# Expert layer of a vision block: tokens as the stationary operand of the second product, in 14 of 16 blocks

## The chip, the cores and the metric

The kernel runs on one core of a Trainium2 chip. The metric is the device time of one execution in microseconds (us), and the time before is the median of three runs, 1112.26 us (1110.14 to 1114.20).

## The reference

Four images of 64 channels and 64x64 pixels go through three layers, each added to or built on the one before:

```python
h = tok(x)                                  # dynamic 3x3 depthwise filter, result (4, 4096, 64)
h = h + attn(layernorm(h))                  # one head over 4096 tokens of width 64, softmax of scores
h = h + ffn(layernorm(h))                   # router picks 1 of 32 experts for each token

# ffn, for all tokens n:
idx = argmax(xf @ router_w.T + router_b)            # E = 32 experts
h   = relu(einsum('nd,ndh->nh', xf, W1[idx]) + b1[idx])    # H = 16 hidden values
out = relu(einsum('nh,nhd->nd', h, W2[idx]) + b2[idx])     # D = 64 values
```

The change is in the last line, the second product of the experts. All is in float32.

## The kernel before, in words

The 16384 tokens are worked on in 16 blocks of 1024 (`BLOCKS`, four to an image). The array is used as four quarters of 64x64 throughout: a helper `rows_of(r)` picks partitions 64r to 64r+63, and the rows (contraction) and columns (output partitions) of a product choose the quarter. In what follows a record is one MATMUL of the trace; a float32 product leaves two records, each with its own LDWEIGHTS, and a bf16 product one.

Attention sets the frame. Each block n has 16 groups g; in each, TensorE makes scores (`score`, L789, 16 records of 64x512), ScalarE takes the exponential (L1009), and TensorE weighs the keys with it (`into_z`, L800, 16 records of 64x512). All other work of TensorE is a list of "fills", named as `o2@7` (fill o2 of block 7), which a hand-written plan (`opening_groups` to `last_groups`) puts at a group of a block. TensorE, ScalarE and VectorE all walk through the same plan in the same order. In `group`, TensorE issues the scores of group g, then the fills of that group, then the weighing of group g-1. The fills of group 16 of a block stand after the last scores of that block and ahead of the first scores of the next one.

All fills of the blocks that the change touches write to one pair of PSUM banks, `both` (128 partitions, 2 banks of 512 float32). A fill waits until the fill before it in that place has been drained (`wait_free`).

The expert layer of a block is a chain of fills. `ot` turns the one-hot choice; `hid0` to `hid3` are the first product, in four slices of 128 of the 32x16 = 512 hidden rows, and stand by hidden row with tokens along the free axis. In blocks 3 to 13 VectorE drains them (L1233) with relu and the mask of the chosen expert; in blocks 0 to 2 ScalarE does (L1001). `o2` is the second product: `w2` and `b2_parts` are stationary, the tokens stream past in runs of 512 columns, and the sums stand by output channel, tokens along the free axis (L763, L771). VectorE adds the two banks into `o2_sb` (L1274, L1278). `fin`, in the next block, is the way back: 16 products with an identity matrix turn 64x64 pieces of `o2_sb` so that tokens lie on partitions (L779). VectorE then does relu and adds the residual (`put_out`, L1201), and SyncE stores the block (`store_block`, L399), waiting for the drain of `fin` (L404). Behind that store on SyncE's queue stand the loads of dynamic filters for a later block (`spread_filters`).

Ahead of blocks 4, 8 and 12 all engines pass a branch, `shift_if_needed` (L860): TensorE waits on several semaphores (L918 to L921), loads a flag and branches on it (L862). In the usual plan `o2@7` and `o2@11` are the last fills ahead of such a branch; ahead of block 4 it is a convolution (`cv@9`, L697).

The last two blocks (14 and 15) have a plan of their own with other PSUM places.

Of the kernel before, what the change touches and what calls it, by code (L numbers as in the profile page):

```python
# [22 lines left out]
BT = QB // 128  # L23
# [62 lines left out]
def at(i, names):  # L86
    return [f"{n}@{i}" for n in names.split()] if 0 <= i < BLOCKS else []
# [53 lines left out]
def third_groups():  # L141
    return {-1: at(1, "z"), 0: at(0, "lg"), 2: at(0, "ot"), 3: at(1, "pz"), 4: [*at(0, "hid0"), *at(6, "sum2 ln")],
            5: at(0, "hid1"), 6: at(0, "hid2"), 7: at(0, "hid3"), 8: at(1, "yt"), 9: at(0, "o2"), 10: at(1, "lg"),
            11: at(6, "xt"), 12: at(6, "g"), 13: [*at(1, "ot"), *at(7, "sum0 sum1")], 14: at(0, "fin"),
            15: at(1, "hid0"), 16: at(1, "hid1")}


def fourth_groups():
    return {-1: at(2, "z"), 0: at(1, "hid2"), 1: at(1, "hid3"), 2: at(2, "pz"), 3: at(1, "o2"), 4: [*at(9, "cc"), *at(7, "sum2 ln")],
            5: at(2, "yt"), 6: at(2, "lg"), 7: at(1, "fin"), 8: at(7, "xt"), 9: at(7, "g"),  # L150
            10: [*at(2, "ot"), *at(8, "sum0 sum1")], 11: at(2, "hid0"), 12: at(2, "hid1"), 13: at(2, "hid2"),
            14: at(2, "hid3"), 15: at(2, "o2"), 16: at(9, "cv")}


def usual_groups(n):

    m, i, j = n - 1, n + NQ, n + NQ + 1
    pair = {4: at(j + 1, "cc"), 7: at(j + 1, "cv")} if j + 1 in PAIRED else {}
    groups = merged({-1: at(m, "z"), 1: at(m - 1, "fin"), 2: at(m, "pz"), 4: at(i, "sum2"), 5: at(m, "yt"),
                     6: at(m, "lg"), 7: at(i, "ln")}, pair,  # L160
                    {8: at(m, "ot"), 9: at(i, "xt"), 10: [*at(i, "g"), *at(j, "sum0 sum1")]})
    if m in CHOSEN_BY_DMA:
        return merged(groups, {12: at(m, "hid0"), 13: at(m, "hid1"), 14: at(m, "hid2"), 15: at(m, "hid3"), 16: at(m, "o2")})
    return groups
# [40 lines left out]
def vit_block_kernel(nc, x, once, kept, out):  # L205
# [6 lines left out]
    with ExitStack() as ctx:  # L212
# [181 lines left out]
        def _(sp):  # L394
# [3 lines left out]

            def store_block(m):  # L399
                fin = f"fin@{m}"  # L400
                if m == BLOCKS - 2:
                    sp.wait_ge(out_ready, 1)
                else:
                    sp.wait_ge(drained[places.of[fin]], places.nth[fin])  # L404
                for half in range(HH):
                    rows = out.rearrange("b (c h q t) w -> b q h c (t w)", c=C, h=HH, q=NQ)
                    sp.dma_start(rows[m // NQ, m % NQ, half, :, :],
                                 out_sb[half * C:(half + 1) * C, m % 2, :, :].rearrange("c t w -> c (t w)")
                                 ).then_inc(out_stored[m % 2], 16)
# [185 lines left out]
        def _(pe):  # L595
# [36 lines left out]
            def from_both(to, weights, tokens, f, start, stop):  # L632
# [5 lines left out]
                                        start=start, stop=stop)  # L638
                return last

            def begin_hidden(full):
                name, i = split(full)
                wait_free(full)
                wait_drained(f"yt@{i}")
                from_both(place[places.of[full]], w1, y_t, int(name[3:]), start=True, stop=False)

            def fill(full):
# [63 lines left out]
                elif name == "g":  # L711
                    if full == "g@0":
                        wait_drained("aw@0")
                    wait_drained(f"xt@{i}")
                    for r in range(2):
                        for c in range(2):
                            cols = slice(0, 512) if i < NQ else half_of(c)
                            last = T.matmul(both[rows_of(c), r, 0:cols.stop - cols.start],  # L718
                                            a_w[rows_of(r), rows_of(c)],
                                            keys_t[rows_of(r), par, q * 512 + cols.start:q * 512 + cols.stop],  # L720
                                            start=True, stop=True)
                    last.then_inc(done, 1)
                elif name == "pz":
                    pe.wait_ge(z_copied, i + 1)
                    for j in range(BT // 2):
                        for c in range(2):
                            for h in range(2):
                                last = T.matmul(both[rows_of(h), c, j * 65:(j + 1) * 65],  # L728
                                                z_sb[rows_of(c), j * 128 + h * 64:j * 128 + h * 64 + 64],
                                                wv_w[rows_of(c), c * 65:(c + 1) * 65], start=True, stop=True)  # L730
                    last.then_inc(done, 1)
                elif name == "lg":
                    wait_drained(f"yt@{i}")
                    for j in range(BT // 2):
                        for r in range(2):
                            for h in range(2):
                                last = T.matmul(both[rows_of(h), r, j * E:(j + 1) * E],  # L737
                                                y_t[rows_of(r), j * 128 + h * 64:j * 128 + h * 64 + 64],
                                                router_w[rows_of(r), :], start=True, stop=True)
                    last.then_inc(done, 1)  # L740
                elif name == "ot":
                    pe.wait_ge(onehot_ready, i + 1)
                    last = turn([onehot[:, t, :, :].rearrange("p u e -> p (u e)") for t in range(BT)], ident_bf)
                    last.then_inc(done, 1)
                elif name.startswith("hid"):
                    f = int(name[3:])
                    wait_drained(f"ot@{i}")
                    if i == BLOCKS - 1 and f == FT - 1:
                        pe.wait_ge(upper_hidden, 1)
                    ahead = full in AHEAD  # L750
                    if i not in CHOSEN_BY_DMA:
                        last = from_both(mine, mask_w, onehot_t, f, start=not ahead, stop=ahead)
                    if not ahead:
                        last = from_both(mine, w1, y_t, f, start=i in CHOSEN_BY_DMA, stop=True)
                    last.then_inc(done, 1)
                elif name == "o2":
                    if i == BLOCKS - 1:

                        pe.wait_ge(upper_hidden, 2)

                    for part in range(2):
                        for r in range(2):
                            T.matmul(mine[rows_of(r), r, :], b2_parts[rows_of(r), part, :], onehot_t[rows_of(r), :],  # L763
                                     start=(part == 0), stop=False)
                    for f in range(FT):
                        wait_drained(f"hid{f}@{i}")
                        if i == BLOCKS - 1:
                            pe.wait_ge(upper_hidden, f + 1)
                        for h in range(2):
                            for r in range(2):  # L770
                                last = T.matmul(mine[rows_of(r), h, :], w2[rows_of(h), f, :], hidden[rows_of(h), f, r, :],  # L771
                                                start=(f == 0 and h != r), stop=(f == FT - 1))
                    last.then_inc(done, 1)
                else:
                    wait_drained(f"o2@{i}")
                    for j in range(4):
                        for r in range(2):
                            for h in range(2):
                                last = T.matmul(both[rows_of(h), r, j * 64:(j + 1) * 64],  # L779
                                                o2_sb[rows_of(r), j * 128 + h * 64:j * 128 + h * 64 + 64],  # L780
                                                ident[rows_of(r), rows_of(r)], start=True, stop=True)
                    last.then_inc(done, 1)
# [301 lines left out]
        def _(dve):  # L1084
# [120 lines left out]
            def drain(full):  # L1205
# [66 lines left out]
                elif name == "o2":  # L1272
                    if i < BLOCKS - 2:
                        V.tensor_copy(o2_sb[:, :], mine[:, 0, :])  # L1274
                        settle()
                    else:
                        dve.wait_ge(lower_copied, i - (BLOCKS - 3))
                    V.tensor_tensor(o2_sb[:, :], o2_sb[:, :], mine[:, 1, :], ALU.add).then_inc(done, 1)  # L1278
                else:
                    put_out(i, both[:, :, 0:256]).then_inc(done, 1)  # L1280

# [133 lines left out]
```

## Time and profile before

| | |
|---|---|
| median of three runs | 1112.26 us (1110.14 to 1114.20) |
| the profiled execution's own time | 1112.06 us |
| its span in the profile | 1110.3 us |
| mean granted TensorE clock | 0.994 of full speed |
| PE busy | 1087.4 us (98%), 12516 matmul records |
| PEld (weight loads, beside PE) | 560.2 us (50%) |
| DVE / ACT / POOL busy | 527.7 / 583.2 / 13.2 us (48% / 53% / 1%) |
| DMA | 63.43 MB, mean 57 GB/s |

How to read it: busy time of an engine is the time in which at least one of its instructions runs, so with four quarters at work a record of 0.59 us may add only 0.11 us. The span is what the profile covers; the profiled execution's own time is 1.8 us more than its span and 0.2 us below the median.

### The profile page before, as it was taken

To read this page: it belongs to the slowest core of one execution; us is meant where nothing else is said; L and a number is where in the kernel's file an instruction comes from. 1 tells how busy PE (TensorE), PEld (TensorE's weight loads), DVE (VectorE), ACT (ScalarE), POOL (GpSimd) and SP (SyncE) were. 2 spreads that over 40 slices of the span, in tenths; PEclk is the share of its full clock that TensorE was granted. 3 is DMA by queue.
4 is the path that set the end of the run, shared out by engine and by line. 5 is a ranking of instruction groups with operands and counts; after the bars stand their busy time and mean duration, and the time that the engine had idled before them with its cause. 6 is when DMAs were issued, how large, how long until landed. Compare 5 with 4: busy or idle time off the path is not lost.

```text
span 1110.3 us, 28800 instructions
## 1 busy us (share of the span) xinstructions
PE 1087.4 (98%) x12516; PEld 560.2 (50%) x12516; DVE 527.7 (48%) x1039; ACT 583.2 (53%) x657; POOL 13.2 (1%) x44
## 2 busy tenths in 40 slices
PE   7899999999999999999999999999999999999997
PEld 4244444555444555555555455555545555554543
DVE  7868765436064553735547364553523131312305
ACT  2466656556555464545546465464645545454543
POOL 3100000000000000000000000000000000000000
PEclk9899999999999999999999999999999999999999
DMA  4845621113025140222313023240100101010000
GB/s 107 198 112 131 135 66 35 40 39 78 5 68 119 39 108 20 62 70 68 83 40 91 19 69 80 47 101 11 39 15 11 42 12 41 11 40 3 12 1 20
DMA packets 23057, 63.43 MB, mean 57 GB/s; under 512 B 3934, under 2 KB 8382, under 8 KB 22540
## 3 DMA queue, kind: packets, MB, share of 16 engines
q1 hardware_dynamic: 22364, 61.26, 23.1%
q8 instruction: 103, 1.69, 0.7%
q10 hardware_dynamic: 560, 0.23, 0.1%
q14 instruction: 30, 0.25, 0.1%
HBM read 52.87 MB, written 5.47 MB: 53 GB/s over the span
## 4 chain that ended last, share of the span: by engine, by line
PE 95%; DVE 2%; issue 1%; DMA 1%; ACT 1%; DVEq 0%; PEld 0%; PEldq 0%; SPq 0%
PE z_ps L800 40%; PE scores L789 38%; PE both L637 5%; PE both L771 4%; PE both L628 2%; PE both L779 1%; PE both L737 1%; PE both L718 1%; PE both L728 1%; PE both L697 1%; PE both L685 1%; DMA filter_ring<-filters 1%; PE both L763 0%; PE scores L637 0%; DVE hres L1173 0%
## 5 line engine op out<-in xcount | busy, mean ns | idle before, releaser
L1009 ACT ACTIVATE probs<-scores 128x1024 f32<-128x1024 f32 x512 | 496.4, 1021 | 464.3 <-PE scores L789 464.3
L789 PE MATMUL scores<-g_t,keys_t 64*64 64x512 f32 x4096 | 513.9, 591 | 2.3 <-ACT g_t L988 1.2
L800 PE MATMUL z_ps<-probs,keys 64*64 64x512 f32 x4096 | 510.5, 591 | 0.0
L789 PEld LDWEIGHTS scores<-g_t,keys_t 64*64 64x64 f32 x4096 | 222.3, 134 | 226.7 <-issue 220.7
L800 PEld LDWEIGHTS z_ps<-probs,keys 64*64 64x64 f32 x4096 | 207.4, 133 | 178.9 <-issue 171.8
L1233 DVE SCALAR_TENSOR_TENSOR hidden<-both,chosen 128x1024 f32<-128x1024 f32 x44 | 53.9, 1225 | 200.6 <-PE both L637 189.3
L1173 DVE TENSOR_TENSOR hres<-hres,tap_product 128x504 f32<-128x504 f32 (+1 forms) x128 | 87.8, 686 | 11.2 <-issue 0.9
L1161 DVE SCALAR_TENSOR_TENSOR tap_product<-filter_ring,w,xin 128x504 f32<-128x504 f32 (+1 forms) x117 | 87.0, 743 | 8.1 <-DMA filter_ring<-filters 4.4
L637 PE MATMUL both<-y_t,w 64*64 64x512 f32 x448 | 61.4, 589 | 0.0
L771 PE MATMUL both<-hidden,w 64*64 64x512 f32 x448 | 56.9, 592 | 0.0
L1274 DVE COPY o_sb<-both 128x512 f32<-128x512 f32 x14 | 9.7, 691 | 85.2 <-PE both L771 85.2
L1191 DVE COPY z_sb<-z_ps 128x512 f32<-128x512 f32 x14 | 9.7, 692 | 68.2 <-PE z_ps L800 68.2
L1141 DVE TENSOR_REDUCE stat<-logits 128x8 f32<-128x256 f32 x16 | 6.7, 420 | 64.2 <-ACT logits L994 64.2
L637 PEld LDWEIGHTS both<-y_t,w 64*64 64x64 f32 x448 | 23.4, 133 | 22.4 <-issue 21.7
L771 PEld LDWEIGHTS both<-hidden,w 64*64 64x64 f32 x448 | 24.1, 133 | 20.5 <-issue 19.7
L1262 DVE RECIPROCAL stat<-both 128x8 f32<-128x8 f32 x16 | 3.3, 208 | 57.4 <-PE both L728 57.4
L1121 DVE TENSOR_TENSOR tap_product<-tap_product 128x512 f32<-128x512 f32 x32 | 22.2, 692 | 2.4
L1123 DVE TENSOR_REDUCE stat<-tap_product 128x8 f32<-128x512 f32 x32 | 21.9, 686 | 2.3
L628 PEld LDWEIGHTS both<-w,keys 64*64 64x64 f32 x512 | 11.5, 134 | 14.8 <-issue 14.8
L779 PEld LDWEIGHTS both<-w,o_sb 64*64 64x64 f32 x512 | 13.2, 134 | 9.4 <-issue 9.4
L628 PE MATMUL both<-w,keys 64*64 64x64 f32 x512 | 11.2, 219 | 6.8 <-DVE keys L1130 6.8
L1201 DVE SCALAR_TENSOR_TENSOR out_sb<-both,h 128x256 f32<-128x256 f32 x30 | 11.3, 420 | 13.1 <-PE both L779 13.1
(162 smaller groups left out, 557.5 us busy)
## 6 DMA issues: line engine op xcount, KB each, us to landing
filter_ring<-filters SPq DMA_DIRECT2D x88, 384.0 KB, 5.4
chosen<-choices SPq DMA_DIRECT2D x44, 256.0 KB
out_dram<-out_sb SPq DMA_DIRECT2D x32, 128.0 KB, 2.4
xin<-x_dram SPq DMA_DIRECT2D x6, 528.0 KB, 9.7
g_t<-g_t SPq DMA_DIRECT2D x24, 128.0 KB, 6.1
hidden<-once_dram SPq DMA_DIRECT2D x1, 930.0 KB, 14.4
chosen<-filters SPq DMA_DIRECT2D x2, 384.0 KB, 6.8
choices<-onehot_t SPq DMA_DIRECT2D x22, 32.0 KB, 1.6
```

The source lines that it names most:

```text
L628: last = T.matmul(both[rows_of(a), h, j * 64:(j + 1) * 64], tiles[2 * j + a][rows_of(h)], ident[rows_of(h), rows_of(h)], start=True, stop= ...
L637: last = T.matmul(to[rows_of(c), r, :], weights[rows_of(r), cols], tokens[rows_of(r), :], start=start, stop=stop)
L771: last = T.matmul(mine[rows_of(r), h, :], w2[rows_of(h), f, :], hidden[rows_of(h), f, r, :], start=(f == 0 and h != r), stop=(f == FT - 1))
L779: last = T.matmul(both[rows_of(h), r, j * 64:(j + 1) * 64], o2_sb[rows_of(r), j * 128 + h * 64:j * 128 + h * 64 + 64], ident[rows_of(r), r ...
L789: last = T.matmul(scores[rows_of(h), c, r * 512:(r + 1) * 512], keys_t[rows_of(r), i // NQ % 2, k * 128 + 64 * h:k * 128 + 64 * h + 64], g ...
L800: last = T.matmul(z_ps[rows_of(c), h, :], keys[rows_of(h), i // NQ % 2, 2 * k + r, :], probs[rows_of(h), (2 * g + c) % RING, r * 512:(r + ...
L1009: A.activation(probs[:, unit % RING, :], scores[:, c, :], ACT.Exp, scale=SCALE).then_inc(probs_ready, 1)
L1121: V.tensor_tensor(squares[:, :, :], centred[:, :, :], centred[:, :, :], ALU.mult)
L1123: V.reduce_sum(total, squares[:, :, :], AX_X)
L1161: return V.scalar_tensor_tensor(dst[:, :, lo:hi], flt, keep["b2c"][:, t:t + 1], pix, ALU.add, ALU.mult)
L1173: V.tensor_tensor(mine[:, :, lo:hi], mine[:, :, lo:hi], dst[:, :, lo:hi], ALU.add)
L1233: V.scalar_tensor_tensor(hidden[:, f, :, :], place[k][:, :, :], 0.0, chosen[:, f, :, :], ALU.max, ALU.mult).then_inc(drained[k], 1)
```

## The change

In blocks 0 to 13 the operands of the second product are swapped. A new function `experts_by_token` makes, for each of 4 token runs j and 2 halves r, first the bias (4 bf16 products, one-hot stationary, `b2_parts` moving, 64 columns) and then 16 float32 products with 64 tokens of `hidden` stationary and `w2` (64 columns) moving. Its sums stand by token in `both`. The fill `fin` goes out of the plan for these blocks. VectorE adds the two banks as before and then calls `put_out` on `o2_sb` at once, and SyncE waits for that through `out_ready`. Blocks 14 and 15 are as they were.

```diff
@@ def third_groups():
-            11: at(6, "xt"), 12: at(6, "g"), 13: [*at(1, "ot"), *at(7, "sum0 sum1")], 14: at(0, "fin"),
-            15: at(1, "hid0"), 16: at(1, "hid1")}
+            11: at(6, "xt"), 12: at(6, "g"), 13: [*at(1, "ot"), *at(7, "sum0 sum1")], 15: at(1, "hid0"), 16: at(1, "hid1")}
@@ def fourth_groups():
-            5: at(2, "yt"), 6: at(2, "lg"), 7: at(1, "fin"), 8: at(7, "xt"), 9: at(7, "g"),
+            5: at(2, "yt"), 6: at(2, "lg"), 8: at(7, "xt"), 9: at(7, "g"),
@@ def usual_groups(n):
-    groups = merged({-1: at(m, "z"), 1: at(m - 1, "fin"), 2: at(m, "pz"), 4: at(i, "sum2"), 5: at(m, "yt"),
+    groups = merged({-1: at(m, "z"), 2: at(m, "pz"), 4: at(i, "sum2"), 5: at(m, "yt"),
@@ def store_block(m):
-                if m == BLOCKS - 2:
-                    sp.wait_ge(out_ready, 1)
+                if m < BLOCKS - 1:
+                    sp.wait_ge(out_ready, m + 1)
@@ TensorE
+            def experts_by_token(i):
+
+
+                def to(bank, c, r, j):
+                    return both[rows_of(c), bank, 256 * r + 64 * j:256 * r + 64 * j + 64]
+
+                def tokens(c, j):
+                    return slice(128 * j + 64 * c, 128 * j + 64 * c + 64)
+
+                for f in range(FT):
+                    wait_drained(f"hid{f}@{i}")
+                for j in range(BT // 2):
+                    for r in range(2):
+                        for part in range(2):
+                            for c in range(2):
+                                T.matmul(to(r, c, r, j), onehot_t[rows_of(r), tokens(c, j)], b2_parts[rows_of(r), part, :],
+                                         start=(part == 0), stop=False)
+                        for f in range(FT):
+                            for h in range(2):
+                                for c in range(2):
+                                    last = T.matmul(to(h, c, r, j), hidden[rows_of(h), f, r, tokens(c, j)],
+                                                    w2[rows_of(h), f, :], start=(f == 0 and h != r), stop=(f == FT - 1))
                 return last
@@ fill o2
+                    if i < BLOCKS - 2:
+                        experts_by_token(i).then_inc(done, 1)
+                        return
@@ VectorE, drain of o2
                     V.tensor_tensor(o2_sb[:, :], o2_sb[:, :], mine[:, 1, :], ALU.add).then_inc(done, 1)
+                    if i < BLOCKS - 2:
+                        settle()
+                        put_out(i, o2_sb[:, :].rearrange("p (r n) -> p r n", r=2)).then_inc(out_ready, 1)
```

## Rows read from the trace of the kernel before

**Rows 1.** The page's part 4, the chain that ended last, by engine.

```profile
PE 95%; DVE 2%; issue 1%; DMA 1%; ACT 1%; DVEq 0%; PEld 0%; PEldq 0%; SPq 0%
```

**Rows 2.** Groups of instructions by form: shapes, count | busy us, mean ns | idle before.

```profile
L771 PE MATMUL both<-hidden,w 64*64 64x512 f32 x448 | 56.9, 592 | 0.0
...
L779 PE MATMUL both<-w,o_sb 64*64 64x64 f32 x512 | 14.0, 220 | 1.6 <-DVE o_sb L1278 1.6
...
L763 PE MATMUL both<-onehot_t,b_parts 64*64 64x512 bf16 x56 | 9.0, 376 | 0.0
```

**Rows 3.** Chain in order of time, 745 to 830 us: start us, us, what.

```profile
759.77 0.17 PE both L763
...
760.20 3.43 PE both L771 x30
...
767.07 1.35 PE scores L789 x15
768.41 0.07 PE both L779 x3
...
769.19 1.78 PE z_ps L800 x16
770.97 1.66 PE scores L789 x15
```

**Rows 4.** Timeline of PE, 740 to 815 us: start us, us, instruction, count.

```profile
781.47 1.98 PE L789 MATMUL scores<-g_t,keys_t 64*64 64x512 f32 x16
783.18 0.67 PE L628 MATMUL both<-w,y_block 64*64 64x64 f32 x30
...
785.37 1.98 PE L789 MATMUL scores<-g_t,keys_t 64*64 64x512 f32 x16
...
792.70 1.98 PE L789 MATMUL scores<-g_t,keys_t 64*64 64x512 f32 x16
...
796.31 1.96 PE L789 MATMUL scores<-g_t,keys_t 64*64 64x512 f32 x16
```

**Rows 5.** Timeline of PE, 334.5 to 338 us, where PE had waited ahead of L628.

```profile
336.82 0.69 PE L628 MATMUL both<-w,keys 64*64 64x64 f32 x32
337.31 1.07 PE L800 MATMUL z_ps<-probs,keys 64*64 64x512 f32 x8
```

**Rows 6.** Waits: who for whom, us in total, times, longest us.

```profile
PEld both L763 <- DVE hidden L1233: 6.1, 11, 0.6
```

**Rows 7.** Timeline of DVE, 758 to 776 us; in brackets the idle time before.

```profile
758.16 1.23 DVE L1233 SCALAR_TENSOR_TENSOR hidden<-both,chosen 128x1024 f32<-128x1024 f32 x1 [3.07 <-PE both L637]
...
767.10 0.69 DVE L1191 COPY z_sb<-z_ps 128x512 f32<-128x512 f32 x1 [1.98 <-PE z_ps L800]
```

**Rows 8.** Chain in order of time, 298 to 304 us, the branch ahead of block 4.

```profile
301.38 0.77 issue
302.15 1.90 PE scores L789 x13
```

**Rows 9.** PE's sequencer (PEldq), one line each, 298 to 304 us: duration, first and last start.

```profile
L921 PEldq EVENT_SEMAPHORE  x2: 51/51/51, 300.3 to 300.4; - x2
```

**Rows 10.** The same of 560 to 570 us, the branch ahead of block 8.

```profile
L921 PEldq EVENT_SEMAPHORE  x2: 51/51/51, 563.7 to 563.8; - x2
...
L809 PEldq EVENT_SEMAPHORE  x1: 51/51/51, 565.4 to 565.4; - x1
```

**Rows 11.** Chain in order of time, 562 to 568 us, the same branch.

```profile
563.02 3.43 PE both L771 x30
```

**Rows 12.** One line of the source, 765 to 770 us: its wait behind fin.

```profile
L819 PEldq EVENT_SEMAPHORE  x1: 51/51/51, 768.8 to 768.8; - x1
```

**Rows 13.** One line of the source, 765 to 770 us: fin's own records.

```profile
L779 PE MATMUL both<-w,o_sb x32: 216/218/268, 768.2 to 769.0; 64*64 64x64 f32 x32
```

**Rows 14.** The page's part 3: the queue of instructions; packets, MB, share.

```profile
q8 instruction: 103, 1.69, 0.7%
```

**Rows 15.** Waits of SyncE's queue.

```profile
SPq L407 <- DVE out_sb L1201: 421.2, 15, 72.2
```

More of the change, by code:

```diff
@@ L639, in from_both @@
                 return last
+            def experts_by_token(i):
[16 more added lines that the diff above has]
+                                                    w2[rows_of(h), f, :], start=(f == 0 and h != r), stop=(f == FT - 1))
+                return last
             def begin_hidden(full):
```

## The prediction

> **What bounds the kernel now.** I read the page's shares first, then the chain that ended last: 95% of the span is TensorE's [rows 1]. The chain in order of time shows why nothing else counts: through a block it goes from one group of matmul records to the next without a hole. So every us of TensorE's stream taken out or put in shows in the time, wherever it stands, and the other engines matter only where they make TensorE wait. I then took the widths of the fills from the timeline and the queue's behaviour from TensorE's sequencer. All is costed against the profiled execution's own time, 1112.06 us (span 1110.3 and 1.8 around it), 0.2 below the median.
>
> **A pace to work with.** A group of 16 attention records takes 1.716 us on the chain; with four quarters at work that is 0.429 us for a 512-column float32 record in its quarter. Scores that begin at 781.47 and 785.37 have between them themselves, one weighing and the 32 float32 records of 64 columns of a turn: 3.90 - 3.43 = 0.47 us [rows 4], or 8 records in each quarter at 0.0585 us, 14.6 ns a record over all. In the same way the 16 bf16 records of 64 columns between 792.70 and 796.31 cost 0.18 us [rows 4].
>
> **1. What goes, 4.34 us a block.** From the end of one weighing at 759.77 to the scores at 770.97 the chain takes 11.20 us and holds four attention groups (6.86), o2 and fin [rows 3]: 4.34 us for the two. It splits into 3.43 of w2 records, 0.43 for two 512-column bf16 records in sequence in two of the quarters (759.77 to 760.20), and 0.47 for fin, a turn like that above. The counts, 448, 56 and 512 records [rows 2] (the last holds blocks 14 and 15 as well), are 32, 4 and 32 a block, and they are the same in all 14 blocks. Gone: 14 x 4.34 = 60.8 us.
>
> **2. What comes, 4.08 us a block.** 8 times (j, r) there are 16 float32 products, 32 records of 64 columns, in the same round of four quarters as a turn: 256 records, 8 x 0.468 = 3.74 us. The bias is 32 bf16 records, 8 in each quarter. Below: 512 bf16 columns take 0.215 us where float32 takes 0.429, so half of 0.0585, 8 x 0.029 = 0.23, total 3.98. Above: 14.6 ns for each of the 288 records whatever its kind, 4.20; two turns of the bf16 kind, 0.36, lie between. I take 0.34: 0.23 and, four times in each quarter, some 0.027 because the float32 weights that follow a bf16 record take longer to load than that record runs. Coming: 14 x 4.08 = 57.1 us. Parts 1 and 2 make -3.7 us, with ends -5.0 and -2.0. The products do the same arithmetic; what is saved is fin and the long bias, and what eats it is that a 64-column record costs a little more than an eighth of a 512-column one.
>
> **3. The waits ahead of it, +0.10 us in 11 blocks.** Before, one wait stood ahead of o2, and its record could sit in the queue with others behind it; TensorE's loads waited up to 0.6 us for VectorE's last hidden drain in all 11 blocks where VectorE drains [rows 6], which ended at 758.16 + 1.23 = 759.39 [rows 7], just before the weighing ran out, so it cost almost nothing. Now five waits stand ahead of the first record. An instruction carries one and the sequencer takes the others, two at a time, so it stands still until 759.4, with an empty queue behind. Where it had stood still before a turn, records came at once and at full pace: 32 from 336.82 to 337.31, 0.49 against 0.47 [rows 5]. Two waits of 0.05 with the gap between them, the load and the start put the first record near 759.67 instead of 759.56. Ends: 0 and 0.25. With 0.10, 11 x 0.10 = 1.1 us. Blocks 0 to 2 have their drains done earlier: nothing.
>
> **4. The branch behind it, +1.65 us twice.** The sequencer runs ahead of the array by a fixed stock of instructions, not of time. Ahead of block 8 it was at the waits of L921 at 563.7 and through the branch at 565.4, while o2's long records ran until 566.45: the branch cost nothing [rows 10, 11]. Ahead of block 4 a shorter fill stood there, the sequencer came to L921 at 300.3, scores began at 302.15, 1.85 later, and the chain has a hole of 0.77 [rows 8, 9]. Behind 64-column records the stock is worth little time: behind fin the sequencer was at its next wait at 768.8, 0.2 before fin's last record started [rows 12, 13]. So ahead of blocks 8 and 12, where o2@7 and o2@11 are the last fills, 1.85 - 0.20 = 1.65 us of hole opens each time, 3.3 us. Ends: 0 (the stock still covers it) and 3.7. Ahead of block 4 nothing changes. At other blocks' starts only one or two waits follow o2, as behind fin, where the stream went on unbroken: nothing.
>
> **5. The rest, nothing.** VectorE's put_out (two instructions of 0.42) moves from behind fin to behind o2; VectorE was idle there for 1.98 us ahead of the z copy at 767.10 [rows 7], and o2's banks are still freed by the add ahead of it. If that cover were gone, the z copy has until pz, a group and a half later. pz now waits for o2 instead of fin, drained long before. On SyncE the store of a block waited for put_out 421.2 us in all [rows 15]; it goes some 4 us earlier, and so may the filter loads behind it, as far as their own wait for free slots (`filters_used`) lets them; they feed VectorE's sums, which don't set the end. More instructions are fetched: 14 x (576 - 136) = 6160 beside some 25000, a quarter more than the 103 packets now [rows 14], one packet in about 1.9 us through the new stretch.
>
> **Sum.** -60.8 + 57.1 + 1.1 + 3.3 = +0.7 us: 1112.8 from the profiled execution, 1113.0 from the median.
>
> **Rivals.**
> *Supply (slower).* The longest run of 64-column records in the trace is 32, which the stock may partly hold; the new one has 288 (576 instructions). If the sequencer or the fetch can't keep 14.6 ns a record, the run goes at its pace. The slowest such run here, fin's on the chain from 768.41 to 769.19, 0.78 us for 32 [rows 3], is 24 ns a record: 288 x 24 = 6.9 us, 14 x (6.9 - 4.34) = +36, with parts 3 and 4 1153 us. It decides from 14.8 ns on: 4.26 us a block make -1.1, with the 4.4 of parts 3 and 4 +3.3, slower by 0.3%. For it: no long run was ever seen, and an instruction packet would have to come in 1.9 us. Against: the run of rows 5 started with the sequencer standing still and still kept the pace; and fin's slowness is a skew that the long bias had left between the quarters (the scores ahead of it count 1.35 on the chain instead of 1.72 [rows 3]). Chance 0.12.
> The Trainium skill, page "TensorE: Matmul & The Clock Gate", section "Wait — 56ns, not 53.3ns?", says that matmuls never start closer than about 25 ns; by it the new stretch would take 7.2 us a block and the kernel 1157 us, as an estimate from that page. The 14.6 ns of [rows 4] contradict it for runs of 32 over four quarters, so I give it no more than the chance of this rival.
> *Upper ends (slower).* The stretch at 4.20 us a block, 0.25 at the start, 1.85 at both branches: -2.0 + 2.8 + 3.7 = +4.5, 1116.8 us. Mechanism: the short stock of instructions, in both places. Chance 0.18.
> *Lower ends (faster).* The bias in its own time, the waits under the skew of the quarters, the sequencer still ahead at the branch: -5.0, 1107.2 us. For it: the branch was hidden at both places before. Against: [rows 8, 12]. Chance 0.17.
>
> **How the numbers follow.** My own case has 0.53. What a measurement tells from no change is about 0.3%, 3.3 us, here 1109 to 1115.6. Faster is the lower ends, 0.17; slower the supply and the upper ends, 0.30; the same 0.53. The range goes from the lower ends, 1107.5, past the upper ends to a supply that is a little short (15.6 ns a record, 4.50 us a block, +6.7), 1119; the likeliest case alone is 1110 to 1115.
>
> **What would show it.** Between the last scores ahead of o2 and the next, the new stretch should be 4.0 to 4.2 us wide, with 256 float32 and 32 bf16 records; L779 should be left with 64 records; the attention groups should keep their 1.716 us. Ahead of blocks 8 and 12 the chain should have an "issue" hole of 1.1 to 1.7 us where it had none, and the first record of the stretch should start 0.1 us after the last hidden drain is through. A stretch over 4.3 us, a hole inside it, or no hole at the branches would make the forecast wrong.

## The result, and the profile after

The changed kernel takes 1157.33 us in the median of four runs (1155.78 to 1160.97), against 1112.77 for the kernel before in the same comparison: a ratio of 1.0399, 95% interval 1.0380 to 1.0418. It is 4% slower; 1113.0 was forecast with a range to 1119. The profiled execution took 1155.78 us (span 1154.0), 43.7 more than that of before. In the kernel after, L655 and L660 are the bias and the products of the new stretch, L815 the scores, L826 the weighing, L888 the branch and L805 the way back that blocks 14 and 15 still have.

One correction to the names in the forecast: a block's plan holds the expert fills of the block before it, so the last fills ahead of the branches of blocks 8 and 12 are o2@6 and o2@10, not o2@7 and o2@11. The places in the traces are the ones that were read; only the numbers were wrong.

First the page's part 4, shares of the chain; it answers to [rows 1].

```profile
PE 92%; issue 3%; DVE 2%; DMA 1%; ACT 1%; PEld 0%; DVEq 0%; PEldq 0%; SPq 0%
```

"issue" is time in which TensorE waited for nothing that the profile shows. It was 1% and is 3%, some 35 us against 11. The groups by form say where (count | busy us, mean ns | idle before), to be laid beside [rows 2]:

```profile
L660 PE MATMUL both<-w,hidden 64*64 64x64 f32 x3584 | 64.6, 221 | 17.5 <-issue 17.5
...
L655 PE MATMUL both<-b_parts,onehot_t 64*64 64x64 bf16 x448 | 26.8, 191 | 4.3 <-issue 4.3
...
L805 PE MATMUL both<-w,o_sb 64*64 64x64 f32 x64 | 1.4, 220 | 1.6 <-DVE o_sb L1304 1.6
```

The counts are the forecast ones (14 x 256 = 3584, 14 x 32 = 448, 64 left of the way back), but inside the new stretch TensorE stood idle for 21.8 us. One stretch on the chain in order of time (start us, us, what), the place that answers to [rows 3]:

```profile
789.06 0.49 PE both L660 x30
789.55 0.01 PE both L655
...
790.08 0.38 PE both L660 x18
790.46 1.45 issue
791.90 0.45 PE both L660 x12
...
792.84 0.07 PE both L660 x3
792.91 1.72 PE scores L815 x14
794.63 1.72 PE z_ps L826 x16
```

Up to 790.08 each unit of 36 records (one pair j, r of the new function: 4 of the bias and 32 of the products) takes 0.51 us, 14.2 ns a record, the forecast pace. Then nothing is issued for 1.45 us, and afterwards the pace is the same again. Every one of the 14 stretches has such a hole, and two have two; from the start of the record before to the start of the record after they measure 1.1 to 1.9 us and 25.2 us in all.

The stretch ahead of block 8 (it stands at o2@6) is one of those with two, and runs into the branch:

```profile
577.33 1.50 issue
...
580.92 1.68 issue
582.60 0.62 PE both L660 x24
...
584.71 3.03 issue
587.74 3.69 PE scores L815 x16
```

From the last product at 583.22 to the first scores at 587.74 are 4.5 us, where the long records of o2 had hidden the branch whole [rows 11]. (The chain lays part of that hole on VectorE's drain of o2, which ran beside it.) The sequencer's branch instruction itself, over the kernel (duration min/median/max; the maximum is the first branch, at 20 us):

```profile
L888 PEldq COMPARE_BRANCH  x4: 342/3640/5274, 20.5 to 862.2; - x4
```

The same of the kernel before:

```profile
L862 PEldq COMPARE_BRANCH  x4: 323/339/4811, 20.2 to 827.0; - x4
```

Before, the three later ones took 0.35, 0.32 and 0.33 us. The one ahead of block 4 is still short now (0.34), the two behind new stretches take 3.5 and 3.7. A clock loss follows both: the scores at 587.74 take 3.69 us instead of 1.72. By stretch (us, busy of PE, PEld, DVE, ACT, POOL, PEclk, DMA):

```profile
588.00:597.00 9.00, 9.00 (x64) 2.85 (x63) 1.38 (x2) 3.99 (x4) 0.00 (x0) 0.74 0.40 90
866.40:875.00 8.60, 8.60 (x68) 3.00 (x72) 1.38 (x2) 3.99 (x4) 0.00 (x0) 0.84 0.01 3
```

TensorE is busy throughout, and the granted clock, 1.00 at these places before, is at its lower level of 1.2 GHz for part of the time: 9.0 x 0.26 + 8.6 x 0.16 = 3.7 us lost, after holes of 4.5 to 5 us that followed stretches which had each stood idle twice.

### The profile page after: what moved, and what is told of

Read it like the earlier page. It is cut to its first block, busy times and chain, and to the rows that moved or that the text cites. A ratio compares the mean times of both kernels' runs of the same rounds, so it can differ in the third digit from the quotient of the medians.

```text
span 1154.0 us, 34976 instructions
## 1 busy us (share of the span) xinstructions
PE 1100.1 (95%) x15596; PEld 484.7 (42%) x15596; DVE 527.1 (46%) x1039; ACT 583.5 (51%) x657; POOL 13.1 (1%) x44
## 4 chain that ended last, share of the span: by engine, by line
PE 92%; issue 3%; DVE 2%; DMA 1%; ACT 1%; PEld 0%; DVEq 0%; PEldq 0%; SPq 0%
PE z_ps L826 38%; PE scores L815 38%; PE both L660 5%; PE both L636 4%; PE both L627 1%; PE both L741 1%; PE both L751 1%; PE both L760 1%; PE both L720 1%; PE both L708 1%; DMA filter_ring<-filters 1%; PE scores L636 0%; DVE hres L1199 0%; PEld both L929 0%; PE z_ps L797 0%
## 5 line engine op out<-in xcount | busy, mean ns | idle before, releaser
L815 PE MATMUL scores<-g_t,keys_t 64*64 64x512 f32 x4096 | 500.1, 596 | 13.1 <-issue 11.9
L826 PE MATMUL z_ps<-probs,keys 64*64 64x512 f32 x4096 | 496.3, 593 | 0.0
L815 PEld LDWEIGHTS scores<-g_t,keys_t 64*64 64x64 f32 x4096 | 172.2, 134 | 282.1 <-issue 267.0
L826 PEld LDWEIGHTS z_ps<-probs,keys 64*64 64x64 f32 x4096 | 161.3, 134 | 229.7 <-issue 199.4
L660 PE MATMUL both<-w,hidden 64*64 64x64 f32 x3584 | 64.6, 221 | 17.5 <-issue 17.5
L660 PEld LDWEIGHTS both<-w,hidden 64*64 64x64 f32 x3584 | 60.5, 134 | 19.3 <-issue 19.3
L655 PE MATMUL both<-b_parts,onehot_t 64*64 64x64 bf16 x448 | 26.8, 191 | 4.3 <-issue 4.3
L636 PEld LDWEIGHTS both<-y_t,w 64*64 64x64 f32 x448 | 18.8, 133 | 27.1 <-issue 26.2
L655 PEld LDWEIGHTS both<-b_parts,onehot_t 64*64 64x64 bf16 x448 | 20.1, 107 | 13.4 <-DVE hidden L1259 7.1
L627 PEld LDWEIGHTS both<-w,keys 64*64 64x64 f32 x512 | 11.0, 139 | 14.4 <-issue 14.4
L1187 DVE SCALAR_TENSOR_TENSOR hres<-filter_ring,w,xin 128x512 f32<-128x512 f32 x15 | 11.3, 756 | 12.4 <-DMA filter_ring<-filters 9.3
```

What stands on the lines that cost most here:

```text
L627: last = T.matmul(both[rows_of(a), h, j * 64:(j + 1) * 64], tiles[2 * j + a][rows_of(h)], ident[rows_of(h), rows_of(h)], start=True, stop= ...
L636: last = T.matmul(to[rows_of(c), r, :], weights[rows_of(r), cols], tokens[rows_of(r), :], start=start, stop=stop)
L655: T.matmul(to(r, c, r, j), onehot_t[rows_of(r), tokens(c, j)], b2_parts[rows_of(r), part, :], start=(part == 0), stop=False)
L660: last = T.matmul(to(h, c, r, j), hidden[rows_of(h), f, r, tokens(c, j)], w2[rows_of(h), f, :], start=(f == 0 and h != r), stop=(f == FT - 1))
L815: last = T.matmul(scores[rows_of(h), c, r * 512:(r + 1) * 512], keys_t[rows_of(r), i // NQ % 2, k * 128 + 64 * h:k * 128 + 64 * h + 64], g ...
L826: last = T.matmul(z_ps[rows_of(c), h, :], keys[rows_of(h), i // NQ % 2, 2 * k + r, :], probs[rows_of(h), (2 * g + c) % RING, r * 512:(r + ...
```

## The experiments

My theory after the two traces (S): the supply of instructions. TensorE's queue of instructions moves packets of 16 KB (q8: 103 packets before, 128 after). 25 more packets for the 6160 more instructions is about 250 in each, so I took a packet for 256; 576 instructions at 7 ns each ask for packets faster than they come. The expectations below call what one packet holds a block of instructions, and where it ends a block boundary. Rivals: a hazard of the new product itself, its sums, banks or waits (H); a floor under the pace (P); packets that happen to be held up by other transfers (D).

**1. A meter: runs of plain products in the kernel before.** The same tile, constant operands, the result overwritten, so no sums and no new waits; only length and width differ.

```diff
+METER = {3: (64, 64), 4: (64, 128), 5: (64, 192), 6: (64, 288), 7: (64, 512), 8: (128, 288), 9: (128, 512),
+         10: (256, 288), 11: (64, 1024), 12: (96, 512), 13: (128, 1024)}     # block: (columns, records)
+                    if i in METER:                                            # ahead of the bias of o2
+                        columns, records = METER[i]
+                        for k in range(records // 8):
+                            for h in range(2):
+                                for c in range(2):
+                                    T.matmul(both[rows_of(c), h, 0:columns], ident[rows_of(h), rows_of(h)],
+                                             w1[rows_of(h), 0:columns], start=True, stop=True)
```

> The kernel before, with runs of plain 64x64 float32 products (constant operands, result overwritten) put ahead of the bias of o2 in blocks 3 to 13; columns and records: 64/64, 64/128, 64/192, 64/288, 64/512, 128/288, 128/512, 256/288, 64/1024, 96/512, 128/1024. Each record is two instructions. Theory S (instruction supply): TensorE holds two blocks of 256 instructions, and one that is asked for when its predecessor is entered can be used about 3.5 us later. Then 64-column records keep 14.6 ns until the second block boundary inside a run and stall 1.7 us there and at each later one: no hole at 64 records, none or one at 128 and 192, one or two at 288, three at 512, seven at 1024 (some 27 us instead of 15). With 96 columns (21 ns a record) holes of about 0.8 us; with 128 columns (28 ns a record, 3.6 us per 256 instructions) next to none whatever the length, with 256 columns none. Rival H (a hazard of the new product: its sums, banks or waits): plain products have none of these, so no holes at any length. Rival P (a floor on the pace of 25 ns a record): no holes, but every 64-column run at 25 ns, 7.2 us for 288.

The timeline of PE in that run (start us, us, line and shapes, count, idle before): the 1024 records of 64 columns, then 1024 of 128 columns.

```profile
957.49 4.01 PE L767 MATMUL both<-w 64*64 64x64 f32 x259
962.86 2.09 PE L767 MATMUL both<-w 64*64 64x64 f32 x128 [1.36 <-issue]
966.33 2.09 PE L767 MATMUL both<-w 64*64 64x64 f32 x128 [1.38 <-issue]
969.80 2.09 PE L767 MATMUL both<-w 64*64 64x64 f32 x128 [1.38 <-issue]
973.27 2.09 PE L767 MATMUL both<-w 64*64 64x64 f32 x128 [1.38 <-issue]
977.29 2.09 PE L767 MATMUL both<-w 64*64 64x64 f32 x128 [1.93 <-issue]
980.76 2.03 PE L767 MATMUL both<-w 64*64 64x64 f32 x123 [1.38 <-issue]
...
1125.69 28.68 PE L767 MATMUL both<-w 64*64 64x128 f32 x1024
```

This is the cause in one view. A hole comes after every 128 records, that is 256 instructions, one packet; from the end of one hole to the end of the next are 3.47 us (once 4.02). With records twice as wide (28.4 us for 1024, 27.8 ns each, 3.55 us for 256 instructions) not one hole opens in 1024 records. The other runs, with holes now measured from the start of the record before to the start of the record after, which is 0.2 us more than the idle time: 64, 128 and 192 records of 64 columns none (0.92, 1.89 and 2.84 us, 14.4 to 14.8 ns each); 288 one of 1.5; 512 three of 1.6, 1.9 and 1.9, 3.74 and 3.75 us apart; 96 columns two of 1.4 and 1.1; 128 columns with 288 and 512, and 256 columns, none. H falls, since plain products do it, and P, since between holes the pace is 14.7 ns. D falls as the main cause too. All that moved while the run of 1024 went on, from 950 to 990 us, were nine instruction packets:

```profile
DMA packets 9, 0.15 MB, mean 4 GB/s; under 512 B 0, under 2 KB 0, under 8 KB 0
## 3 DMA queue, kind: packets, MB, share of 16 engines
q8 instruction: 9, 0.15, 1.4%
```

I had expected seven holes and got six, since the first two boundaries of the run passed free instead of one; the next hole, 128 records on, fell into the bias of o2 right behind the run (1.06 us of idle time at 983 us).

**2. The same stretch in three pieces.** In 11 blocks the units stand at three groups, with attention between them.

```diff
+PIECES = {"outa": range(0, 3), "outb": range(3, 5), "o2": range(5, 8)}     # units (j, r)
+    late = {0: at(m - 1, "outb"), 1: at(m - 1, "o2")} if m - 1 in CHOSEN_BY_DMA else {}
-        ... 16: at(m, "o2")
+        ... 16: at(m, "outa")
```

> The changed kernel, but in blocks 3 to 13 the eight units of the new product are made in three pieces of 3, 2 and 3 units (216, 144 and 216 instructions), at group 16 of the block and groups 0 and 1 of the next, with two attention groups between pieces. Same products, same instructions, same waits. Theory S: no piece holds two block boundaries, so the holes of 1.1 to 1.9 us go in these 11 blocks (13 holes, about -20 us), the holes at the branches ahead of blocks 8 and 12 and the low clock behind them shrink (about -10 us and more), and the three early blocks keep theirs: about 1125 us. Rival H: the holes stay where the sums or banks make them, about 1157. Rival D (transfers that happen to delay single packets): holes stay at random places, above 1150.

Measured: 1126.91 us, ratio 1.0120 (1.0096 to 1.0145), so 30 us less than the whole stretch for the same instructions. All 13 holes of those 11 blocks are gone. Ahead of block 8 the chain reads:

```profile
572.49 0.49 PE both L662 x31
572.99 2.23 issue
575.22 3.64 PE scores L819 x16
```

The branch instruction took 1.25 us there, 0.92 more than the 0.33 it takes at best, so the rest of the hole, 1.3 us, is the short stock of my step 4 (forecast 1.65), now seen without the supply on top. Ahead of block 12 the same sum gives 1.3 again (a hole of 2.68, a branch of 1.70). The scores behind it again take twice their time.

**3. The changed kernel without the branches.**

```diff
-                    shift_if_needed(b)          # TensorE, ahead of blocks 4, 8 and 12; ScalarE and VectorE alike
```

> The changed kernel without the guard ahead of images 2 to 4 (the branches of blocks 4, 8 and 12 on all engines are left out; the work that they skip is skipped anyway). Theory S: the 16 holes inside the stretches stay (some 24 us), the holes behind the stretches of blocks 7 and 11 (4.8 and 5.0 us) go, with them the two spells of half clock behind them (about 3 us each) and the 2.4 us hole in block 4: about 1139 us. My forecast's step on the branch (1.65 us twice): 1154. Rival: the low clock comes from the stretches and not from the branch holes: about 1145.

The first branch, at 20 us, stays. Measured: 1136.80 us, ratio 1.0228 (1.0195 to 1.0262), 20.5 us less than with them; the four runs lie between 1134.54 and 1141.07, so this is good to a few us. The holes in the stretches stayed (16 again, at other records, since the packets' boundaries moved); mean clock of the profiled run 0.995 instead of 0.986. So a third to a half of the loss of 44.6 us is the branches with what hangs on them, far more than the 3.3 us of the forecast.

**4. The product over all 128 partitions.** Half as many float32 products, two halves of the array side by side.

```diff
+                        for part in range(2):
+                            for c in range(2):
+                                T.matmul(to[c], onehot_t[:, tokens[c]], b2_tall[:, r, part, :], start=(part == 0), stop=False)
+                        for f in range(FT):
+                            for c in range(2):
+                                last = T.matmul(to[c], hidden[:, f, r, tokens[c]], w2[:, f, :], start=False,
+                                                stop=(f == FT - 1))
```

> The second product with tokens stationary as in the change, but with all 128 partitions as the contraction (a tile of 128 rows by 64 columns), so that 16 products of a unit become 8, and the two banks need no adding. 192 records instead of 288 (384 instructions instead of 576), each two records of a column half side by side. Theory S: the array needs 128 records x 29 ns = 3.74 us and 64 x 15 for the bias, 4.1 to 4.7 us, and in 3.7 us of it only 256 instructions are used, so the supply just keeps up: holes of 0 to 0.5 us instead of 1.1 to 1.9; with the branches some 1118 to 1128 us. Rival P or H: the stall goes with the change of operands and stays, above 1145. If records of this shape run at 0.117 us in place of 0.0585, 3.7 us more a block, about 1165.

I had miscounted: a unit has 16 + 4 records, so there are 160 and 320 instructions, not 192 and 384. Measured: 1128.39 us, ratio 1.0146 (1.0122 to 1.0170). The float32 part of a unit on the chain:

```profile
769.33 0.49 PE both L663 x16
769.82 0.06 PE both L660 x4
769.88 0.49 PE both L663 x16
```

Half as many records in the same 0.49 us, no hole in any of the 14 stretches: what stalls is the count of instructions in a time, not the arithmetic. But the bias takes longer in this form, the whole is 4.5 us wide and gains nothing on the 4.34 of before, blocks without a branch behind them are 0.47 us longer than before, and behind it the branches still stalled (3.1 and 2.3 us for the instruction).

**5. Blocks 6 and 10 as before, the others changed.** Three kernels: the pieces of 2 in blocks 3 to 5, 7 to 9 and 11 to 13, with 0 to 2 as before too; whole stretches in all 12; the product of 4 in all 12.

```diff
+BY_TOKEN = (3, 4, 5, 7, 8, 9, 11, 12, 13)                                    # pieces
+BY_TOKEN = tuple(i for i in range(BLOCKS - 2) if i not in (6, 10))           # whole; 128 partitions
```

> The new product in three pieces (3, 2 and 3 units) in nine blocks (3 to 5, 7 to 9, 11 to 13); the second product and the way back as before in blocks 0 to 2 and in blocks 6 and 10, whose fills stand ahead of the branches. Theory S: no hole anywhere, no branch hole: what is left is the array's own side of my forecast, -0.2 us a block, so about 1111 us, 0.997 to 1.000 of before. If the pieces cost at their edges (a wait, a skew) what they save, 1113. If splitting only hides part of the stall, 1120 or more.

> The changed kernel, whole stretches, but blocks 6 and 10 as before, so that 3.5 us of long records stand ahead of the branches of blocks 8 and 12. Theory S: saved are both stretches (6.8 us), both branch holes (9.5) and the half clock behind them (some 6): about 1135 us. Rival (the branch holes come from where the block boundaries happen to fall, not from the stretch ahead): only the 6.8 us go, about 1150.

> The product over all 128 partitions in 12 blocks, blocks 6 and 10 as before. In the run with all 14 its stretch had no hole but was 4.47 us wide and more with the bias, and blocks without a branch took 64.72 us against 64.25 before. Theory S: the branch holes (4.05 and 3.1 us) go, 12 x 0.47 us stay: about 1118 us. If the holes at the branches stay, 1125.

Whole stretches: 1138.12 us, ratio 1.0221 (1.0203 to 1.0240), 19 us saved by two blocks out of 14; 22 had been expected, and some 7 if the stretch ahead of a branch had no part in its hole. Over 128 partitions: 1119.64, ratio 1.0058 (1.0041 to 1.0075). Pieces: 1111.37 us over 12 runs, ratio 0.9988 (0.9978 to 0.9999), the only version that is not slower than the kernel before; it is 0.1% faster, which barely leaves the interval. Its chain at one block shows the array's side of the forecast free of the supply:

```profile
629.22 0.04 PE both L661 x2
...
630.80 1.72 PE scores L823 x16
632.52 1.71 PE z_ps L834 x16
634.24 0.03 PE both L661 x2
...
635.26 1.72 PE scores L823 x16
636.98 0.03 PE both L661 x2
...
638.53 1.62 PE z_ps L834 x11
```

The pieces take 1.58, 1.02 and 1.55 us: 4.15 for 288 records, where 4.08 was forecast for the stretch and 4.34 stood before.

The later branches of this kernel took 0.22 to 0.35 us. In the kernel with whole stretches they took 0.35, 1.07 and 0.33, in that over 128 partitions 0.35, 1.22 and 0.33, and in the meter the one ahead of block 8 took 3.52 and opened a hole of 3.05 us, although 3.5 us of o2's long records stood between it and the run of 288. So a fast stretch makes a long branch likely, and a packet's boundary at the wrong place can, it seems, still do it without one right ahead. That the kernel before had three short ones may in part be luck of where its boundaries fall; I have not moved its boundaries alone to prove it.

## Why the prediction was wrong

**Step 1, what goes (4.34 us a block): right.** The way back is gone from the trace, and most blocks of the kernel in pieces are shorter by 0.22 us than those before, where steps 1 and 2 make 0.26.

**Step 2, what comes (4.08 us, ends 3.98 and 4.20): right for the array.** 4.15 us in pieces; in the whole stretches it is 4.1 to 4.3 us once the hole is taken off.

**Step 3, the waits ahead (+0.10): nothing.** As at 786.97 on the chain, the stretch follows what stands ahead of it without a hole in all 14 blocks. The five waits are all on one semaphore, and in blocks 3 to 13 the trace has only one instruction of the sequencer ahead of the stretch, with two waits, and one more wait at the first weight load.

**Step 4, the branch (+1.65 twice): right mechanism, wrong size.** 1.3 us is what the short stock costs (experiment 2). On top the branch itself took 3.2 and 3.4 us more than at best, and behind the holes the clock fell, 3.7 us. Ahead of block 4, where nothing was to change, a hole of 1.83 us opened just behind the branch. These make some 15 us; taking the branches out gave 20.5 (experiment 3). Of the rest, 0.8 is the hole that the kernel before has too at the branch of block 4 [rows 8], and in the profiled runs 3.2 us of the difference stand in the opening, ahead of the first branch taken out. So the branches cost 15 to 20 us, not 3.3.

**Step 5 and the rival "supply": the step that failed.** "One packet in about 1.9 us through the new stretch" stood there as costing nothing, and the rival that doubted it had a chance of 0.12. Its price, 1153 us, came near, but for another reason than the one I gave it: I let it slow every record to 24 ns, by the record pace of a fill whose slowness was skew, while the pace stays at 14.2 ns (14.7 in the meter) and the time goes in whole holes, 25.2 us in 16 of them. And what I held against it, [rows 5], proved nothing on supply: the 64 instructions of a turn pass one boundary at most. The number that decided was in the forecast, 1.9 us a packet; what was missing was how long a packet takes to be of use. The trace before would have given a warning: packets came some 10 us apart, nowhere were 128 records made in less than 5.6 us, and where two packets followed each other most closely, behind the branches of blocks 8 and 12, they started 3.5 and 3.4 us apart.

**The sum.** In start-to-start times, profiled run against profiled run: 25 us of holes in the stretches; 9.6 from the last product to the next scores at the two branches (4.8 and 5.0, against none); some 2 at the branch of block 4; 3.7 of low clock behind the branches; -1.4 to -2.7 for the array's own gain. That makes 38 to 39 of the 43.7. Another 2 us stand in the opening, where the mean clock from 30 to 70 us was 0.84 instead of 0.90. They need not come from the change: the kernel in pieces of experiment 5, whose blocks 0 to 2 are as before, is 2.5 us longer in the opening too. The remaining 3 to 4 us, in blocks 4, 9 and 14 above all, I have not placed.

**A right total with a wrong mechanism.** The Trainium skill, page "TensorE: Matmul & The Clock Gate", section "Wait — 56ns, not 53.3ns?", with its floor of 25 ns between matmuls would have given 1157 us, the measured time to the us, and is still not the cause: between holes the records start 14.7 ns apart in runs of 128 (experiment 1). A right total is no proof of the mechanism. The page of the Trainium skill that does bear on it is "Runtime: NRT & Kernel Launch", section "Instruction fetch mechanics": instructions come in blocks of 16 KiB (256), fetched one ahead while the current one runs. The traces agree with the block (a hole per 128 records of two instructions). The same section of the Trainium skill says that the fetch is mostly hidden, because the sequencer dispatches more slowly than it fills; here it is not, at 7.4 ns an instruction (14.7 for a record of two). And it says that a taken branch whose target lies outside the two blocks at hand forces a fetch; the long branches of 3.5 and 3.7 us fit that, against 0.33 for a short one, but no run here moved a branch's target alone.

## What to carry to other kernels

Count instructions per time as well as columns per time: in the runs of this kernel TensorE could use 256 instructions in less than about 3.5 us (13.7 ns each) only for the length of one packet or two, and beyond that a hole followed at every further packet, of some 3.5 us less the time that the packet's instructions ran. The 3.5 is an estimate between the 3.47 us of the run with holes and the 3.55 of the run without. So many small float32 products, four instructions each, should be spread between long ones in pieces of fewer than 256 instructions, or made with a larger contraction so that one instruction does more. And nothing fast should stand right ahead of a branch: the sequencer's lead is a number of instructions, and what was hidden behind 3.5 us of long records costs its time behind short ones (1.3 us here, and with a long branch 4.5 to 4.7).

## What the runs showed of the hardware that was not expected

- At full demand 256 instructions take 3.47 us, holes included, four times of five in the run of 1024 records (once 4.02), 3.74 and 3.75 in the run of 512 and 3.74 in the run with 96 columns. Only packets of instructions moved in all three, so why the longer ones are longer is open. Records of 128 columns show no hole at 3.55 us per 256.
- The first boundary or two of a run pass free: in the meter the first hole came after 159, 180 and 259 records of 64 columns and after 298 of 96, the later ones every 128. That the sequencer was ahead there, or that these packets were asked for in the slow part, is my reading and not shown.
- A tile of 128 rows by 64 columns takes as long per column half as one of 64 by 64 (0.49 us for 16 records instead of 32), so it halves the instructions of the float32 part at no cost on the array.
- The clock fell to 1.2 GHz behind the idle times at the branches of 4.5 and 4.7 us in the changed kernel, 2.2 and 2.7 in experiment 2 and 4.0 in experiment 4 (in the first two kernels the scores behind took up to 3.69 and 3.64 us instead of 1.72). It also fell once without a branch, in the kernel with whole stretches of experiment 5, behind a stretch that had stood idle for 1.32 and 1.97 us: 14 records of the scores at 648 us took 3.34 us. It did not fall behind 3.07 us at block 12 in experiment 4, 3.05 at block 8 in the meter, or the meter's six holes in a row of 1.4 to 1.9. The length of a hole alone doesn't decide it.
